# Attention and mixture-of-experts layer on one core: later pair sums in odd units, two sums moved from GpSimd to VectorE, projections counted by halves, one score product moved forward

## The reference

```python
def reference(x, ...):
    x = _L0_conv_ref(x, ...)      # 1x1 convolutions, a 32 x 32 channel attention, residual
    t = _to_tokens(x)             # 1024 tokens of 256 features
    t = t + _L1_attn_ref(_ln_t(t), ...)
    t = t + _L1_ffn_ref(_ln_t(t), ...)   # shared expert + 2 of 8 experts, hidden 128
    return _from_tokens(t, x)

# of _L1_attn_ref: 8 heads of 32 features, two softmax maps a head
a1 = jax.nn.softmax(jnp.einsum('bhqd,bhkd->bhqk', q1, k1) / scale, axis=-1)
a2 = jax.nn.softmax(jnp.einsum('bhqd,bhkd->bhqk', q2, k2) / scale, axis=-1)
attn = a1 - lam.reshape(1, H, 1, 1) * a2
o = jnp.einsum('bhqk,bhkd->bhqd', attn, v)
# then a group norm over 4 groups of 64 features x 1024 tokens, and out_w
```

## Time and profile before

| what | value |
|---|---|
| median of 3 runs | 5967.44 (5963.66 to 5967.70) |
| the profiled execution | 5965.52, span of the core 5963.7 |
| PE busy | 5762.7 (97%) |
| DVE busy | 5002.4 (84%) |
| ACT busy | 3258.7 (55%) |
| POOL busy | 2957.8 (50%) |
| granted TensorE clock, mean | 0.994 |
| longest waits for another engine's work inside attention | ACT L579 for PE L1363, 1220.1; POOL L423 for DVE L930, 396.2 |

### The profile page before, as it was taken

One profiled execution on the slowest core, in us unless ns is written; L12 is line 12 of the kernel. 1 busy time (PEld: TensorE's weight loads), 2 busy tenths in 40 slices (PEclk: granted clock), 3 DMA queues, 4 the chain that ended last, 5 costly groups with the idle time before them and its releaser, 6 DMA issues.

```text
span 5963.7 us, 117362 instructions
## 1 busy us (share of the span) xinstructions
PE 5762.7 (97%) x39472; PEld 3674.9 (62%) x39472; DVE 5002.4 (84%) x6839; ACT 3258.7 (55%) x5868; POOL 2957.8 (50%) x1334
## 2 busy tenths in 40 slices
PE   6999999999999999999999999999999999999999
PEld 4566565655657556575665756657566575665656
DVE  5978879798897988979889798897978979788797
ACT  4645546455564655646556465564655646555464
POOL 3816538074380744708347183561825628266281
PEclk9999999999999999999999999999999999999999
DMA  2212222122222222222222221222212222122221
GB/s 78 59 48 62 60 55 54 56 58 58 53 52 62 54 58 55 49 61 58 57 55 50 63 58 55 55 51 63 60 49 56 50 63 59 49 60 50 65 59 47
DMA packets 148810, 338.00 MB, mean 57 GB/s; under 512 B 38624, under 2 KB 61280, under 8 KB 139744
## 3 DMA queue, kind: packets, MB, share of 16 engines
q1 hardware_dynamic: 146400, 329.26, 22.7%
q10 hardware_dynamic: 1792, 1.12, 0.1%
HBM read 90.49 MB, written 17.30 MB: 18 GB/s over the span
## 4 chain that ended last, share of the span: by engine, by line
PE 79%; DVE 10%; issue 6%; DMA 2%; ACT 2%; SPq 0%; DVEq 0%; ACTq 0%
PE psum L1141 18%; PE psum L1363 16%; PE psum L1285 15%; PE psum L1306 14%; PE psum L1460 7%; DVE minus_max L834 5%; PE psum L1313 4%; PE psum L1193 1%; PE psum L1332 1%; PE psum L1414 1%; PE psum L1291 1%; DMA prob_sums<-combine_rows_dram 1%; DMA stack<-stage 1%; DVE small L749 1%; DVE small L886 1%
## 5 line engine op out<-in xcount | busy, mean ns | idle before, releaser
L579 ACT ACTIVATE probs<-psum 128x512 f32<-128x512 f32 x4096 | 2215.8, 595 | 1249.8 <-PE psum L1363 1220.1
L423 POOL TENSOR_TENSOR prob_sums<-prob_sums,probs 128x1024 f32<-128x1024 f32 x960 | 2288.2, 2383 | 475.6 <-DVE prob_sums L930 396.2
L834 DVE TENSOR_REDUCE minus_max<-psum 128x1 f32<-128x1024 f32 x2048 | 2397.8, 1206 | 145.7 <-PE psum L1285 132.7
L1363 PE MATMUL psum<-stack 98*128 98x512 f32 x4096 | 1439.1, 431 | 3.5 <-DVE max_rows L844 3.5
L1285 PE MATMUL psum<-stack 96*128 96x512 f32 x4096 | 1219.4, 406 | 39.7 <-DVE minus_max L834 28.9
L1306 PE MATMUL psum<-probs,v_tokens 128*32 128x256 f32 x16384 | 1112.3, 387 | 0.0
L393 POOL TENSOR_TENSOR stage<-probs,stage 128x512 fp32r<-128x512 f32 x16 | 20.7, 1295 | 2130.9 <-ACT probs L545 2130.9
L1363 PEld LDWEIGHTS psum<-stack 98*128 98x128 f32 x4096 | 712.1, 189 | 541.4 <-ACT probs L579 331.6
L1285 PEld LDWEIGHTS psum<-stack 96*128 96x128 f32 x4096 | 713.8, 189 | 324.5 <-DVE minus_max L834 143.5
L1306 PEld LDWEIGHTS psum<-probs,v_tokens 128*32 128x32 f32 x16384 | 453.0, 110 | 468.1 <-issue 227.4
L423 POOL TENSOR_TENSOR prob_sums<-probs 128x1024 f32<-128x1024 f32 x240 | 573.9, 2391 | 273.3 <-ACT probs L579 273.3
(11 more groups left out here) (162 smaller groups left out, 5163.7 us busy)
## 6 DMA issues: line engine op xcount, KB each, us to landing
stack<-stage SPq DMA_DIRECT2D x1024, 128.0 KB, 3.0
stack<-stage SPq DMA_DIRECT2D x256, 256.0 KB, 3.1
prob_sums<-combine_rows_dram SPq DMA_DIRECT2D x128, 256.0 KB, 3.8
stage<-combine_rows_dram SPq DMA_DIRECT2D x128, 256.0 KB, 3.3
x_tile<-x_dram SPq DMA_DIRECT2D x34, 512.0 KB, 3.6
x_tile<-o_head SPq DMA_DIRECT2D x480, 32.0 KB, 1.9
y_dram<-residual SPq DMA_DIRECT2D x16, 512.0 KB, 2.8
y_dram<-stage SPq DMA_DIRECT2D x16, 512.0 KB, 2.9
```

The lines of the kernel that those rows point to most:

```text
L423: nc.gpsimd.tensor_tensor(total, first, probs[:, k % NP, :], ALU.add).then_inc(sum_pool, 1)
L579: nc.scalar.activation(probs[:, k % NP, half * HALF:(half + 1) * HALF], ps[:, exp_bank(k) + half, :], ACT.Exp).then_inc(p_ready, 1)
L834: v.tensor_reduce(nm[:, u % 2, q:q + 1], flat_in, AX.X, ALU.max, negate=True).then_inc(ring_free, 1)
L1363: mm(ps[:, exp_bank(k) + half, :], stack[0:KS, s, 1, kt * P:(kt + 1) * P], stack[0:KS, s, 0, half * HALF:(half + 1) * HALF], start=True, s ...
```

## The change

1. *Pair sums.* In odd units from 3 on, `pair_sum(u)` stands behind the maximum of tile 6, not 5.
2. *Unit 14.* Tiles 6 and 7 of unit 14 (`BY_DVE`) are added by DVE (`last_sum(14, 1, 6)` and `(14, 1, 7)`); POOL makes no addition behind its third one there. `norm_sums(0)` moves from unit 15 to unit 14, behind the pair sum. ACT waits for `sum_dve` from the tile that takes the buffer of tile 6 on. `norm_groups(0)` keeps its place.
3. *Projection halves.* A new semaphore `proj_half` counts the first halves; ACT takes half 0 when that is made, half 1 when the whole is.
4. *Unit 0.* PE makes one score product of pair 1 (tile 6 of unit 1) ahead of the second-kind product of tile 2, and `weighted(0, 0)` behind it.

```diff
+BY_DVE = ((UNITS - 2) * NT + 6, (UNITS - 2) * NT + 7)
 ADDED = [u * NT + kt for u in range(UNITS - 1) for group in sum_groups(u) for kt in group[1:]
-         if kt != sum_groups(u)[1][1]]
-LAST_ADDED = [kt for group in sum_groups(UNITS - 1) for kt in group[1:]]
+         if kt != sum_groups(u)[1][1] and u * NT + kt not in BY_DVE]
+LAST_ADDED = list(BY_DVE) + [(UNITS - 1) * NT + kt for group in sum_groups(UNITS - 1) for kt in group[1:]]
...
-FIRST_VALUES_AT = ((0,), (1, 2), (3, 4), (5, 6))
+FIRST_VALUES_AT = ((), (1, 2), (3, 4), (5, 6))
...
-NORM_AT = (UNITS - 1, 0)
+NORM_AT = (UNITS - 1, 1)
...
-                    act.wait_ge(ring_full, b * len(RING) + RING_AT["proj", t] + 1)
                     for half in range(NH):
+                        if half:
+                            act.wait_ge(ring_full, b * len(RING) + RING_AT["proj", t] + 1)
+                        else:
+                            act.wait_ge(proj_half, b * 3 + t + 1)
                         take_projection(t, half, 0, wide(RING_AT["proj", t] % 2)[:, half, :])
...
-                            if k - NP >= (UNITS - 1) * NT:
-
-                                act.wait_ge(sum_last, b * len(LAST_ADDED) + last_adds(kt - NP))
+                            if k - NP >= BY_DVE[0]:
+
+                                act.wait_ge(sum_dve, b * len(LAST_ADDED) + last_adds(k - NP))
...
-                    dve.wait_ge(ring_full, b * len(RING) + n + 1)
+                    if item[0] != "proj":
+                        dve.wait_ge(ring_full, b * len(RING) + n + 1)
...
-                    if u < UNITS - 1 and kt == 5:
+                    if u < UNITS - 1 and kt == (6 if u % 2 and u >= 3 else 5):
                         pair_sum(u)
+                    if u == UNITS - 2 and kt == 5:
+                        norm_sums(0)
+                    if u == UNITS - 2 and kt == 6:
+                        last_sum(u, 1, 6)
                     if u == UNITS - 1 and kt == NT - 2:
-                        last_sum(1, 5)
+                        last_sum(u, 1, 5)
                     if u and kt == HEAD_AT:
                         head_out(u - 1)
+                    if u == UNITS - 2 and kt == 7:
+                        last_sum(u, 1, 7)
...
-                    if kt == group[1]:
+                    if u < UNITS - 1 and kt == group[2]:
+                        dve.wait_ge(sum_pair, b * (UNITS - 1) + UNITS - 1)
+                    elif kt == group[1]:
                         dve.wait_ge(ones_done, b * ONES + n - NS + 1)
...
-                        if (u, pair) == NORM_AT:
-                            norm_sums(0)
...
+                            if half == 0:
+                                last.then_inc(proj_half, 1)
...
+                            if k == 2:
+                                ring_step(BESIDE[u, pair][0])
                             for half in range(NH):
...
+                            if k == 2:
+                                weighted(0, 0)
+                            for item in BESIDE[u, pair][slice(int(k == 2), 2) if kt % 2 == 0 else slice(2, None)]:
                                 if item[0] != "turn":
                                     ring_step(item)
-                        if (u, pair) == (NORM_AT[0], NORM_AT[1] + 1):
+                        if (u, pair) == NORM_AT:
                             norm_groups(b, 0)
```

More of the change, by code:

```diff
@@ L73, in adds @@
     u, kt = divmod(tile, NT)
-    if u == UNITS - 1:
+    if u == UNITS - 1 or tile in BY_DVE:
         return len(ADDED)
@@ L77, in adds, with last_adds @@
     return sum(at <= u * NT + upto for at in ADDED)
-def last_adds(kt):
-    upto = max([kt] + [group[1] for group in sum_groups(UNITS - 1) if kt == group[0]])
-    return sum(at <= upto for at in LAST_ADDED)
+def last_adds(tile):
+    u, kt = divmod(tile, NT)
+    upto = max([kt] + [group[1] for group in sum_groups(u) if kt == group[0]])
+    return sum(at <= u * NT + upto for at in LAST_ADDED)
 def ones_after(u, pair):
@@ L243, in build @@
         st_full, p_ready, pv_done = sem("st_filled"), sem("probs_ready"), sem("pv_done")
-        sum_pool, sum_pair, sum_last = sem("sum_by_pool"), sem("pair_sum_by_dve"), sem("last_sum_by_dve")
+        proj_half = sem("projection_half")
+        sum_pool, sum_pair, sum_dve = sem("sum_by_pool"), sem("pair_sum_by_dve"), sem("sum_by_dve")
         ones_done = sem("ones_done")
@@ L943, in beside_score, with last_sum @@
                         sum_recips(u - 1, 0)
-                    if u < UNITS - 1 and kt == 5:
+                    if u < UNITS - 1 and kt == (6 if u % 2 and u >= 3 else 5):
                         pair_sum(u)
+                    if u == UNITS - 2 and kt == 5:
+                        norm_sums(0)
+                    if u == UNITS - 2 and kt == 6:
+                        last_sum(u, 1, 6)
                     if u == UNITS - 1 and kt == NT - 2:
-                        last_sum(1, 5)
+                        last_sum(u, 1, 5)
                     if u and kt == HEAD_AT:
                         head_out(u - 1)
+                    if u == UNITS - 2 and kt == 7:
+                        last_sum(u, 1, 7)
                     if u == UNITS - 1 and kt == NT - 1:
                         head_statistics(HEADS - 2)
-                def last_sum(g, kt):
-                    u, group = UNITS - 1, sum_groups(UNITS - 1)[g]
+                def last_sum(u, g, kt):
+                    group = sum_groups(u)[g]
                     n, k = u * GROUPS + g, u * NT + kt
@@ L958, in last_sum @@
                     dve.wait_ge(p_ready, b * 2 * UNITS * NT + 2 * k + 2)
-                    if kt == group[1]:
+                    if u < UNITS - 1 and kt == group[2]:
+                        dve.wait_ge(sum_pair, b * (UNITS - 1) + UNITS - 1)
+                    elif kt == group[1]:
                         dve.wait_ge(ones_done, b * ONES + n - NS + 1)
                     else:
-                        dve.wait_ge(sum_last, b * len(LAST_ADDED) + last_adds(kt) - 1)
+                        dve.wait_ge(sum_dve, b * len(LAST_ADDED) + last_adds(k) - 1)
                     first = probs[:, (k - 1) % NP, :] if kt == group[1] else total
-                    v.tensor_tensor(total, first, probs[:, k % NP, :], ALU.add).then_inc(sum_last, 1)
+                    v.tensor_tensor(total, first, probs[:, k % NP, :], ALU.add).then_inc(sum_dve, 1)
                 def k2_low_part():
@@ L988, in _ @@
                             beside_score(u, at)
-                        if (u, pair) == NORM_AT:
-                            norm_sums(0)
                         if u == UNITS - 1:
                             for g, at in (((0, 1),), ((0, 2),), ((1, 4),), ())[pair]:
-                                last_sum(g, at)
+                                last_sum(u, g, at)
                 norm_variance(0)
@@ L1236, in _ @@
                 first_back(0, half)
-            first_projection(0, 0)
+            first_projection(0, 0).then_inc(proj_half, 1)
             def tokens(n):
@@ L1317, in add_up @@
                 def add_up(u, g):
-                    if u == UNITS - 1:
-                        pe.wait_ge(sum_last, b * len(LAST_ADDED) + last_adds(sum_groups(u)[g][-1]))
+                    last = u * NT + sum_groups(u)[g][-1]
+                    if last in LAST_ADDED:
+                        pe.wait_ge(sum_dve, b * len(LAST_ADDED) + last_adds(last))
                     else:
-                        pe.wait_ge(sum_pool, b * len(ADDED) + adds(u * NT + sum_groups(u)[g][-1]))
+                        pe.wait_ge(sum_pool, b * len(ADDED) + adds(last))
                     ones_mm(u, psums[:, (u * GROUPS + g) % NS, :], g == len(sum_groups(u)) - 1).then_inc(ones_done, 1)
@@ L1365, in attention @@
                                    stop=True).then_inc(st_full, 1)
-                            for item in BESIDE[u, pair][slice(0, 2) if kt % 2 == 0 else slice(2, None)]:
+                            if k == 2:
+                                weighted(0, 0)
+                            for item in BESIDE[u, pair][slice(int(k == 2), 2) if kt % 2 == 0 else slice(2, None)]:
                                 if item[0] != "turn":
                                     ring_step(item)
-                        if (u, pair) == (NORM_AT[0], NORM_AT[1] + 1):
+                        if (u, pair) == NORM_AT:
                             norm_groups(b, 0)
@@ L1503, in behind_attention @@
                 pe.wait_ge(f_hid, b * NH * NE + NH * NE - 1)
-                first_projection(b + 1, 0)
+                first_projection(b + 1, 0).then_inc(proj_half, 1)
                 down(NH * NE - 1)
```

## The result

| | median | range | runs |
|---|---|---|---|
| before | 5966.09 | 5963.41 to 5971.54 | 20 |
| after | 5975.56 | 5972.88 to 5980.39 | 20 |

The ratio is 1.0015, 95% interval 1.0009 to 1.0022: 9.5 slower, where 5933 was forecast, 33 faster than this median, and outside the range of 5898 to 5954.

The account below looks back on a forecast made before the run. PE, busy 97% of the span, was taken as the bound, with POOL setting the pace in units 8 to 14. Gains of 5.6 + 19.2 + 9.6 = 34.4 gave 5933, range 5898 to 5954.

Parts of the forecast that it names:

- the term on the moved pair sums: Odd units' pair sums one maximum later: POOL lags 1.7 at unit 14, leaving 0.35 of 2.0; 5.6 gained in all.
- rival 3: Each moved pair sum costs POOL 1.14, ACT falls back, lag 4.6; 37 slower, 6004; chance 0.06.
- What bounds the kernel: PE is busy 97% of the span; in units 8 to 14 POOL sets the pace through the pair sum.
- Norm sums and second group of unit 14: Unit 14: norm_sums(0) moved there, DVE adding tiles 6 and 7; add_up(14, 1) 2.0 earlier, before POOL's lag.
- The wait for POOL: Unit 15: PE idles 2.12 for norm_sums(0), as DVE instructions using SBUF alone stand still while POOL adds.
- Clock: Behind norm_groups(0) in unit 15, with little idle time, the clock stays up: 12 x 1.6 = 19.2 gained.
- Projection halves: Before attention: ACT takes projection 1's first half early; first score product 0.6 earlier, 9.6 gained in all.
- Unit 0 forward: Unit 0's score product ahead: 0.6 earlier, 0.4 through in units 1 and 2, 0.2 left after unit 3's moved sum.
- Rival 1: Port rule is all: POOL's lag doesn't reach unit 14; 5906, or 5864 if DVE's gain reaches PE; chance 0.20.
- rival 2: The clock falls all the same, with some 1 us of idle time; 19.2 missing, 5952; chance 0.14.
- rival 4: The projection half is hidden: DVE or ACT still sets the first maximum; 9.6 less, 5943; chance 0.08.
- The list of what would show it: Trace signs: right if clock 1.00 and odd pair sums 1.2; wrong if ACT waits for POOL in units 8 to 14.

## Why the prediction was wrong

**The step that failed** is the term on the moved pair sums: "A maximum takes DVE 1.14" and "I take 0.3 for each of units 9, 11 and 13", with a lag of 1.7 at unit 14 and 0.35 left of the 2.0. The lag of POOL's fourth addition, from the start of attention:

| unit | 7 | 9 | 11 | 13 |
|---|---|---|---|---|
| prediction | 0.9 | 1.2 | 1.5 | 1.8 |
| measured | 1.98 | 2.78 | 3.53 | 4.35 |

Three things were missing, and all can be read in traces.

1. *The length of the delay.* The sum comes 1.57 later, not 1.14: it started 0.85 behind the exponential it needs, and now starts 2.42 behind it. Behind the maximum of tile 5 DVE was ahead of PE, and the pair sum filled that time. Now DVE waits for PE's next product instead (0.36 at 644.86) and makes the sum afterwards. The prediction took the place of the sum from DVE's own times and didn't ask whether the next maximum's input was there.
2. *The other side of the wait.* ACT takes a buffer of `probs` again when POOL has added it. Before, the exponential of tile 3 of an even unit started 1.17 behind POOL's last addition of the unit before it, now 0.11 behind it: that slack of 1.1 is smaller than the 1.57. So POOL's delay goes through ACT to PE, and the next odd unit's sum is later still. "A late rest shortens the wait" is the opposite of what happens: the rest is late because of the wait, and the lag grows by 0.8 for each odd unit. The prediction named this wait only in rival 3, at 0.06, and set it down as POOL's 1.14 in full.
3. *Unit 3.* The prediction let its moved sum take 0.2 of the gain made in unit 0. It took 0.8: in unit 6 POOL is 0.4 late, and 0.4 early with the sums put back. That 0.4 of lag and the 1.57 of unit 7 make up the 1.98.

**The sum closes with the measured terms.** `add_up(14, 1)` 2.3 later: 16 x 2.3 = 37 slower. The clock: 20 faster. The halves: 9 faster (in this trace the part outside attention is 0.55 a batch shorter than before). 37 - 20 - 9 = 8 slower; measured 9.5. The forecast had 5.6, 19.2 and 9.6, all as gains: the first term accounts for 5.6 + 37 = 43, all of the error.

Step by step:

- *What bounds the kernel*: right. That POOL sets the pace in units 8 to 14 is shown by the 38 that the short third addition gains, with the sums at their old place.
- *Norm sums and second group of unit 14*: right for the kernel in which POOL isn't late. 2.0 was forecast; the version alone gives 1.9. It needs the pair sum to stand behind POOL's third addition: in the kernel after the sum comes first, and the norm sums' copy waits for the third addition behind it.
- *The wait for POOL*: too general. "A DVE instruction that reads and writes SBUF alone stands still while POOL adds" holds for the copy, the third norm sum and the pair sum. It doesn't hold for the statistics of a head, from SBUF to SBUF as well, which take 0.41 at 644.78, inside POOL's additions from 642.49 to 647.32, and 0.43 at 702.67 with POOL idle.
- *Clock*: right in size, 19.2 forecast, 20 measured with unit 14 alone. The reason given, "as it does in the four batches", was none, since PE idles 2.1 in these too. In the kernel after it holds with another idle time than forecast: the 0.35 didn't come, but the idle time is 1.2 at `add_up(14, 0)` and no longer 2.1 at norm_groups(0).
- *Pair sums*: wrong, above. DVE's gain of 0.65 is real in units 3, 9, 11 and 13 (1.22 for 1.88), and is paid with 1.1 in even ones.
- *Projection halves*: right in size (0.55 to 0.60 a batch for 0.6), on condition that the clock stays up. Alone they shorten the part outside attention by 0.45 and gain nothing in all. ACT takes the two halves apart, at 448.23 and 449.63, as the step has it.
- *Unit 0 forward*: right where the sums aren't moved. Of 0.4 a batch, 0.3 comes through by the medians (5.3 in one pair of versions, 4.7 in the other) and 0.4 in attention by the traces.
- *Rival 3* was the mechanism, with ACT falling back. Its lag of 4.6 was measured as 4.35, its 2.5 for `add_up(14, 1)` as 2.3. That these agree so well is in part luck: it had four times 1.14, and the lag is 0.4, 1.57 and then 0.8 three times. Its 6004 had the clock falling in all batches (26 of it), which didn't happen. *Rival 1* is refuted by the 2.33 of even units and the lag of 4.35, *rival 2* by the clock of 1.00, *rival 4* by the 0.60 that the halves gain with the clock up.
- The list of what would show it held in most lines: clock 1.00, sums of 1.2 in odd units and over 2 in four even ones, 3.57 of idle time in unit 7 (3.1 forecast), no idle time ahead of the first score product. The norm sums' copy of 2.32, not 0.17, and ACT waiting for POOL in units 8 to 14 spoke for rival 3.

The Trainium skill ("SBUF — State Buffer", section "Who interferes with whom") says that where a DVE and a GpSimd instruction both need the shared port pair, the one that starts first keeps it for the whole instruction and the other is blocked. The trace agrees in both directions: the pair sum of unit 12 takes 1.1 longer beside POOL, and POOL's third addition of unit 14 takes 0.8 longer beside the pair sum. The rule tells which one waits. What the freed time is worth, against the wait of a third engine for the buffer, it leaves open.

The best version that makes all the sums is the change with the pair sums put back: 5896, 1.1% faster than before (0.9888), and 79 under the kernel after. The one with a product of its own for a tile of unit 8 isn't told from it.

## What to carry to other kernels

A delay of an instruction has to be read at both ends: when its inputs will be there at the new place (the engine may have been filling a gap with it), and how much slack each waiter has, through the whole ring of buffers. If the ring closes on itself, here POOL, ACT, PE, DVE, POOL, the part beyond the slack comes back in each round, and in these runs it was gone only where POOL had idle time and ACT had slack (unit 5), not behind unit 3. A gain that leans on an instruction's place against another engine's (the norm sums behind POOL's third addition) is gone when another part of the same change moves that engine.

## What was not expected of the hardware

- PE idle for 1.2 at `add_up(14, 0)` left the clock at 2.4 GHz in all 16 batches; idle for 2.1 at norm_groups(0) brought 1.2 GHz in 12 of 16. Idle for 1.2 and, 5 later, for 1.1 again (the moved sums alone), it was 2 of 16. With the idle time of 2.1 as before, small shifts elsewhere changed the count: 8 of 16 with the product of unit 0 forward, and with the projections 0.45 a batch shorter 13 of 16, in nine of them for 6.8 and not 3.4. Why stays open.
- DVE stands still for 0.38 to 0.40, put down to issue, in each batch of the two versions that have the unit 14 part without the halves, and for 0.03 in those with both: an edit at a batch's start moved a term at its end by 0.34.
